# Key halves summed by GpSimd, first loads reordered, stacked rows copied by two engines, second memory projected at a norm

## The reference

```python
def layer0_and_3(x, memory):                     # own weights each
    mp = memory @ W_mem.T                        # memory projection, 256 x 256
    c = softmax(x @ mp.T / sqrt(256)) @ mp
    g = sigmoid(concat(x, c) @ W_gate.T + b_gate)
    return rmsnorm(x + g * c) * norm_w
def layer1(x, ctx):                              # vm: mask that picks expert v or l
    h = rmsnorm(x); q, k, v = split(where(vm, h @ v_qkv, h @ l_qkv))
    x += where(vm, A @ v_dense, A @ l_dense)     # A: causal attention, 16 heads of 16, rotary q, k
    x += cross_attention(rmsnorm(x), ctx)        # 16 heads of 8
    x += where(vm, mlp_v(rmsnorm(x)), mlp_l(rmsnorm(x)))    # 688 hidden
def layer2(x, ctx):
    x += tanh(g1) * latent_attention(layernorm(x), ctx)     # 16 heads of 64, masked keys
    x += tanh(g2) * gelu(layernorm(x) @ W1) @ W2            # 1024 hidden
```

## Time and profile before

| | |
|---|---|
| median of 3 runs | 793.43 us |
| profiled execution | 791.2 us |
| its span | 789.3 us |
| PE, DVE, ACT, POOL busy | 709.3, 387.7, 360.7, 8.6 us |
| mean granted PE clock | 0.95 of full |
| PE's share of the chain that ended last | 79% |

### The profile page before, as it was taken

How to read it: one execution, slowest core, us unless ns; L and a number is a source line. 1 busy time by engine, 2 the same in 40 slices (tenths; PEclk the granted TensorE clock), 3 DMA queues, 4 the chain that set the end, 5 groups by cost and what they waited for, 6 DMA issues and landing times.

```text
span 789.3 us, 13530 instructions
## 1 busy us (share of the span) xinstructions
PE 709.3 (90%) x5816; PEld 557.7 (71%) x5816; DVE 387.7 (49%) x798; ACT 360.7 (46%) x716; POOL 8.6 (1%) x12
## 2 busy tenths in 40 slices
PE   4788898898999999999886979987999999999995
PEld 3667675557987777678774867654689867776893
DVE  0645826637824644152356284366276455433414
ACT  3413453477322566545253245535564345665433
POOL 0010000000000000000001000000000000000000
PEclk9979999599999999999997989979899999999999
DMA  8302000021021000400400020001020400000000
GB/s 323 157 0 81 2 2 28 2 75 74 1 81 81 1 1 2 160 21 7 167 27 1 1 81 2 2 27 56 19 74 1 161 1 2 1 2 1 1 0 27
DMA packets 6555, 34.57 MB, mean 44 GB/s; under 512 B 1504, under 2 KB 2784, under 8 KB 4960
## 3 DMA queue, kind: packets, MB, share of 16 engines
q1 hardware_dynamic: 5056, 26.85, 9.0%
q10 hardware_dynamic: 1440, 6.86, 2.4%
HBM read 32.66 MB, written 1.05 MB: 43 GB/s over the span
## 4 chain that ended last, share of the span: by engine, by line
PE 79%; DVE 10%; ACT 8%; issue 1%; DMA 1%; SPq 0%; ACTq 0%; DVEq 0%
PE ps_B L842 7%; PE ps_A L842 7%; PE ps_B L631 4%; PE ps_A L631 3%; PE ps_B L807 3%; PE ps_A L807 3%; PE ps_B L913 2%; PE ps_A L913 2%; PE ps_B L644 2%; PE ps_A L644 2%; PE ps_A L963 2%; PE ps_B L597 2%; PE ps_B L951 2%; PE ps_A L951 2%; PE ps_B L963 2%; PE ps_B L989 2%
## 5 line engine op out<-in xcount | busy, mean ns | idle before, releaser
L1530 DVE TENSOR_REDUCE max_A<-ps_A 128x2 f32<-128x512 f32 x64 | 39.9, 685 | 23.2 <-PE ps_A L770 13.1
L1530 DVE TENSOR_REDUCE max_B<-ps_B 128x2 f32<-128x512 f32 x64 | 40.4, 685 | 22.0 <-PE ps_B L770 17.0
L631 PE MATMUL ps_B<-q_B,kz_B 128*128 128x256 f32 x264 | 36.8, 299 | 2.2 <-DVE kz_B L1455 1.7
L631 PEld LDWEIGHTS ps_B<-q_B,kz_B 128*128 128x128 f32 x264 | 34.2, 199 | 4.1 <-DVE kz_B L1455 1.9
L807 PE MATMUL ps_B<-q_B,kz_B 64*128 64x256 f32 (+1 forms) x320 | 32.1, 310 | 5.5 <-ACT big_B L1236 2.9
L1232 ACT ACTIVATE big_B<-ps_B,key_bias_B 128x256 f32<-128x256 f32 x64 | 25.0, 474 | 21.5 <-PE ps_B L818 21.5
L1067 ACT ACT_TABLE_LOAD x27 | 34.6, 1283 | 0.5
L1236 ACT ACTIVATE big_B<-ps_B 128x384 f32<-128x384 f32 (+1 forms) x48 | 23.6, 544 | 24.5 <-PE ps_B L818 24.4
L842 PE MATMUL ps_B<-big_B,v_B 128*32 128x256 f32 (+2 forms) x320 | 34.3, 396 | 0.0
L631 PE MATMUL ps_A<-q_A,kz_A 128*128 128x256 f32 x264 | 33.2, 286 | 0.9 <-DVE kz_A L1455 0.8
L807 PEld LDWEIGHTS ps_B<-q_B,kz_B 64*128 64x128 f32 (+1 forms) x320 | 23.5, 194 | 14.9 <-ACT big_B L1236 5.4
(11 more groups left out here) (351 smaller groups left out, 1574.5 us busy)
## 6 DMA issues: line engine op xcount, KB each, us to landing
ffn_w<-in_l1m SPq DMA_DIRECT2D x2, 3072.0 KB, 13.3
ffn_w<-in_l2f SPq DMA_DIRECT2D x2, 3072.0 KB, 9.7
attn_w<-in_l1a SPq DMA_DIRECT2D x2, 2048.0 KB, 9.4
v_B<-in_l1d ACTq DMA_DIRECT2D x2, 1408.0 KB, 5.7
v_A<-in_l1d ACTq DMA_DIRECT2D x2, 1408.0 KB, 5.7
attn_w<-in_l2q SPq DMA_DIRECT2D x2, 1024.0 KB, 4.9
attn_w<-in_l2q SPq DMA_DIRECT2D x4, 512.0 KB, 4.6
v_A<-in_gm SPq DMA_DIRECT2D x2, 640.0 KB, 6.4
```

The costliest lines, as they stand in the source:

```text
L631: last = mm(out, weights(a)[:, at:at + P], L.x_part(i, b), start=(t == 0), stop=(t == len(terms) - 1))
L1530: last = nc.vector.tensor_reduce(mx[:, :, h], L.ps[:, h % 4, :].rearrange("p (q k) -> p q k", q=ST), AX.X, ALU.max)
```

## The change

1. **Key halves.** For cross and latent attention POOL adds the two key halves of each head's exponentials (128 x 256 float32, both inputs in SBUF) into a spare tile (`key_sums`: `xv`, `xl`, and for cross also `xn` and `big2`). `weigh` then has one sum matmul a head in place of two, and waits for POOL's adds between the value matmuls and the sum matmuls. There are 32 adds for a lane and pass. POOL gets an order list, and its memsets stand in it. Self attention stays as it is.
2. **First loads.** Lane A's context, the projection part of the first memory's weights (128 KB, a transfer of its own) and A's sequence go first; const comes fourth; then B's context and sequence, the gate weights, positions and `trig`, which now go into `ffn_w`. One-hot, rotary matmuls and ACT's three copies are moved behind lane A's first norm. The waits for them move to `rotate` and `stack_self`, and the load of the experts' weights into `ffn_w` waits for them.
3. **Stacked rows.** ACT copies banks 0 and 1 of q and k, DVE banks 2 and 3.
4. **Second memory.** `memory_projection(L, 1)` and ACT's `memory_save(L, 1)` come before `sum_squares(L, 5)`, the norm of the GELU layer, and wait for `added(4)`; `ffn_up` waits for the copies, `gm_scores` for `added(5)`.
5. **Orders.** The lists of PE, ACT and DVE are written anew. Lane A's memory stage opens pass 0; from self attention on lane B leads in pass 0 as before, but now it also leads through the experts and latent attention and opens pass 1.

```diff
 (ORDER: PE, ACT and DVE lists replaced)
+    "POOL": [
+        0, 1, 2, 17, 16, 8, 8, 9, 9, 1, 17, 16, 8, 8, 8, 8],
...
+            def key_sums(self, a, i):
+                n = i % (2 * TILES[a])
+                if n < 4:
+                    return self.chunk((self.xv, self.xl)[n // 2], n % 2)
+                return self.chunk(self.xn, n - 4) if n < 6 else self.chunk(self.big2, n - 4)
...  (SP)
+            context(A, 0)
+            memory_weights()
+            sequence(A, 0)
+            sp.dma_start(const[:], const_d).then_inc(const_in.sem, 16)
+            context(B, 0)
+            sequence(B, 0)
+            gate_weights()
+            (positions, then trig into ffn_w, on trig_in)
...
+                else:
+                    sp.wait_ge(trig_ready.sem, 1)
                 sp.dma_start(ffn_w[:], l1m_d).then_inc(weights_in["l1m"].sem, 16)
...  (POOL)
+                def add_halves(L, block):
+                    a, h0, heads = BLOCKS[block]
+                    n0 = a * HEADS + h0
+                    for i in range(heads):
+                        b = i // TILES[a]
+                        if i % TILES[a] == 0 and b >= 2:
+                            wait(*L.pv_done.at(it, BLOCK_BASE[block] + b - 1))
+                        wait(*L.probs_ready.at(it, n0 + i + 1))
+                        p = L.weights(a, i)
+                        nc.gpsimd.tensor_tensor(L.key_sums(a, i), p[:, 0:S], p[:, S:2 * S], ALU.add)\
+                            .then_inc(L.halves_added.sem, 1)
+                        yield
...  (PE, weigh)
-                        for part in range(2):
+                        for part in range(2 if a == SELF else 1):
...
+                        if a != SELF:
+                            pe.wait_ge(*L.halves_added.at(it, n0 - HEADS + (b + 1) * tiles))
+                            for j in range(tiles):
+                                last = mm(strip(j, 1, 0), sums(a, order[b * tiles + j]), L.key_sums(a, b * tiles + j),
+                                          start=False, stop=final, skip_group_check=True)
                         last.then_inc(L.pv_done.sem, 1)
...  (ACT, stacked_self)
-                        for b in range(4):
+                        for b in range(2):
...  (DVE, new, after self_lo)
+                def stacked_self(L):
+                    for tile, stacked, saved in ((L.q[:], L.q_stacked, L.q_ready),
+                                                 (L.kz[:, 0:8 * S], L.k_stacked, L.k_saved)):
+                        dve.wait_ge(*stacked.at(it, 1))
+                        tiles = tile.rearrange("p (c b s) -> p b c s", c=2, b=4)
+                        for b in range(2, 4):
+                            nc.vector.tensor_copy(tiles[:, b], L.ps[:, b, :].rearrange("p (c s) -> p c s", c=2))\
+                                .then_inc(saved.sem, 1)
+                            yield
...  (PE, order of a lane)
+                yield from memory_projection(L, 0)
                 yield from gated_memory(0)
                 yield from sum_squares(L, 0)
+                if it == 0 and L.t == 0:
+                    yield from rotary_tables(L)
...
                 yield from layer_norm_sum(L, 1)
+                yield from memory_projection(L, 1)
                 yield from sum_squares(L, 5)
```

More of the change, by code:

```diff
@@ L182, in build @@
         tanh_gates = sb("tanh_gates", 2)
-        weights_in = {n: signal(f"weights_in_{n}") for n in ("gm0", "gm1", "l1a", "l1c", "l1m", "l2kv", "l2q", "l2f")}
+        weights_in = {n: signal(f"weights_in_{n}") for n in ("gm0", "gm1", "gm0_mem", "l1a", "l1c", "l1m", "l2kv", "l2q", "l2f")}
         const_in = signal("const_in")
         onehot_ready = signal("onehot_ready")
+        trig_in = signal("trig_in")
         trig_done = signal("trig_done")
@@ L232, in __init__ @@
                 self.stat = m("stat", 8)
-                self.inputs_in = s("inputs_in")
+                self.inputs_in = s("inputs_in", 16)
+                self.ctx_in = s("ctx_in", 16)
                 self.down_in = s("down_in", 16)
@@ L296, in __init__ @@
                 self.head_out = s("head_out", 11)
+                self.halves_added = s("halves_added", 32)
                 self.added_done = s("added_done", 5)
@@ L506, in wait, with batch @@
                 pool.sem_inc(pool_waits.sem, 1)
-            for it in range(PAIRS):
-                for L in lanes:
-                    if it:
-                        wait(*L.pv_done.at(it - 1, 16))
-                    nc.gpsimd.memset(L.mask_row[:].bitcast(F32), 0.0).then_inc(L.rows_cleared.sem, 1)
-                for L in lanes:
-                    wait(*L.sq_ready.at(it, 1))
-                    nc.gpsimd.memset(L.v[:, 0:V_AT[LATENT]], 0.0).then_inc(L.v_cleared.sem, 1)
+            def batch(L, it):
+                def add_halves(L, block):
[10 more added lines that the diff above has]
+                        yield
+                if it:
+                    wait(*L.pv_done.at(it - 1, 16))
+                nc.gpsimd.memset(L.mask_row[:].bitcast(F32), 0.0).then_inc(L.rows_cleared.sem, 1)
+                yield
+                wait(*L.sq_ready.at(it, 1))
+                nc.gpsimd.memset(L.v[:, 0:V_AT[LATENT]], 0.0).then_inc(L.v_cleared.sem, 1)
+                yield
+                for block in (1, 2, 3):
+                    yield from add_halves(L, block)
+            weave(ORDER["POOL"], *(chain(*(batch(L, it) for it in range(PAIRS))) for L in lanes))
         @block.tensor
@@ L521, in _, with rotary_tables @@
             mm = nc.tensor.matmul
-            pe.wait_ge(const_in.sem, 80)
-            pe.wait_ge(onehot_ready.sem, 1)
-            for half, table in enumerate((T_COS, T_SIN)):
-                for c in range(ST):
-                    last = mm(lanes[0].half(0, half), lanes[1].big[:, table + c * P:table + (c + 1) * P],
-                              lanes[0].chunk(lanes[0].big, c), start=(c == 0), stop=(c == ST - 1))
-            last.then_inc(trig_done.sem, 1)
+            def rotary_tables(L):
+                pe.wait_ge(trig_in.sem, 32)
+                pe.wait_ge(onehot_ready.sem, 1)
+                for half, table in enumerate((T_COS, T_SIN)):
+                    for c in range(ST):
+                        last = mm(L.half(0, half), ffn_w[:, table + c * P:table + (c + 1) * P],
+                                  onehot[:, c * S:(c + 1) * S], start=(c == 0), stop=(c == ST - 1))
+                last.then_inc(trig_done.sem, 1)
+                yield
             def batch(L, it):
@@ L1053, in _, with rotary_tables @@
             act.dma_start(constb[:], constb_d.bitcast(BF16)).then_inc(const_in.sem, 16)
-            act.wait_ge(const_in.sem, 80)
+            act.wait_ge(const_in.sem, 48)
             fn(tanh_gates[:], vec[:, VEC_GATES:VEC_GATES + 2], ACT.Tanh).then_inc(tanh_ready.sem, 1)
-            act.wait_ge(trig_done.sem, 1)
-            fn(cos[:], lanes[0].half(0, 0), ACT.Copy)
-            fn(fast[:], lanes[1].big[:, T_FAST:T_END], ACT.Copy)
-            fn(sin[:], lanes[0].half(0, 1), ACT.Copy).then_inc(trig_ready.sem, 1)
+            def rotary_tables(L):
+                act.wait_ge(trig_in.sem, 32)
+                fn(fast[:], ffn_w[:, T_FAST:T_END], ACT.Copy)
+                act.wait_ge(trig_done.sem, 1)
+                fn(cos[:], L.half(0, 0), ACT.Copy)
+                fn(sin[:], L.half(0, 1), ACT.Copy).then_inc(trig_ready.sem, 1)
+                yield
             step = Steps(act, act_step)
@@ L1285, in gated_memory @@
                     yield from gm_sigmoid(L, g)
+                yield from memory_save(L, 0)
                 yield from gated_memory(0)
                 yield from rstd(L, 0)
+                if it == 0 and L.t == 0:
+                    yield from rotary_tables(L)
                 yield from rstd(L, 1)
@@ L1316, in batch @@
                 yield from w1_hi(L, 1)
+                yield from memory_save(L, 1)
                 yield from rstd(L, 5)
@@ L1334, in _, with rotary_onehot @@
             stt = nc.vector.scalar_tensor_tensor
-            dve.wait_ge(const_in.sem, 80)
-            for c in range(ST):
-                last = ts(lanes[0].chunk(lanes[0].big, c), pos_i[:], const[:, K_IOTA:K_IOTA + 1], float(c * P),
-                          ALU.subtract, ALU.is_equal)
-            last.then_inc(onehot_ready.sem, 1)
+            def rotary_onehot():
+                dve.wait_ge(trig_in.sem, 32)
+                for c in range(ST):
+                    last = ts(onehot[:, c * S:(c + 1) * S], pos_i, const[:, K_IOTA:K_IOTA + 1], float(c * P),
+                              ALU.subtract, ALU.is_equal)
+                last.then_inc(onehot_ready.sem, 1)
+                yield
+            dve.wait_ge(const_in.sem, 48)
             def lines(tile, n, cols=S):
@@ L1622, in batch @@
                 yield from self_lo(L)
+                yield from stacked_self(L)
                 yield from all_maxima(0)
```

61 lines of the change are left out of this document (38 added, 23 removed), and 43 rows, old and new, of the table ORDER.

## The result

The changed kernel takes **783.48 us** (median, 782.51 to 783.83, 4 runs); the kernel before took 794.58 beside it. The ratio is **0.986, 95% interval 0.982 to 0.990**: 11 us faster, where 28.4 were forecast. The time lies above the forecast's range (756 to 779).

The account below looks back on a forecast made before the run. PE work was taken as the bound in most stretches, DVE's maxima in some. The terms 7 + 15.4 + 5 - 1 + 2 = 28.4 us took 791.2 to 762.8; with the median 2.2 higher, 765 us, range 756 to 779.

Parts of the forecast that it names:

- price of an add: POOL's 128x256 add of two SBUF inputs in cross and latent attention: 0.7 us, between 0.43 and 0.93.
- Latent, 15.4 us forecast: Latent attention: halved sum matmuls save PE 0.48 us in each of 32 steps, all counted, 15.4 us.
- Cross, 5 us forecast: Cross attention: halved sum matmuls save 0.44 us in each of 16 steps, 7.0 us, of which 5 counted.
- The cover: Cross attention: two adds have 1.66 us before their sums are wanted, 0.83 us each, less the signals.
- Rival A: POOL keeps latent but loses cross, by adds of 0.9 to 1.1 us or adds waiting for DVE; 771 us, chance 0.10.
- Rival B: POOL paces cross and latent steps and becomes the bound, slower than before; up to 840 us, chance 0.04.
- Rival C: Less PE work and a new wait lower the clock in more cross stretches; 775 us, chance 0.09.
- Rival D: The early start is absorbed by gate weights, masks or rotary insertion; other edits give 21.4; 772 us, chance 0.07.
- First loads, 7 us forecast: Start: first scores near 9 us instead of 17.11, 8 us sooner, less 1 us for rotary tables; gain 7.
- The rotary insertion: Start: one-hot, four rotary matmuls and three ACT copies between the first lane's two norms cost 1 us.
- Second memory, 2 us forecast: End of each pass: projection moved to the last layer norm gains 1 us per pass, 2 in all.
- Stacked rows, -1 us forecast: Row stacks copied by ACT and DVE: a loss of 1 us, ends +3 and -5, from DVE copies in maxima.

Follow-up runs that it names:

- latent_halves: The changed kernel with key halves for latent attention only, cross having its four sum matmuls a head pair on PE again; 778.20 us, ratio 0.9815.
- dve_adds: The changed kernel with key halves for latent only, its 64 adds on DVE instead of POOL, cross without halves; 774.51 us, ratio 0.976.
- adds_unused_cross: one_half with only the 64 cross adds put back on POOL, their results used by nobody; 775.19 us, ratio 0.979.
- one_half: The changed kernel without POOL's adds or PE's wait for them, one sum matmul a head over the first key half; 768.75 us, ratio 0.969.
- adds_unused: one_half with the 128 POOL adds put back, their results used by nobody and PE not waiting; 782.14 us, ratio 0.988.
- late_clear: The changed kernel with POOL's first clears of the value tiles put behind DVE's one-hot table; 779.32 us, ratio 0.982.
- only_halves: The kernel before with the key halves alone, cross and latent, in its own orders with a fitted POOL list; 781.15 us, ratio 0.985.

## Why the prediction was wrong

**The step that failed** is "price of an add", not by its number but by what it was a price of. An undisturbed add took 0.71 us, where I took 0.7, and PE's waits for POOL came to 1.4 us. I asked only whether the add would be late for PE, and put its effect on DVE and on the clock at nothing in the sum. There the cost fell, 13 us by ratio (0.969 to 0.986): DVE's operations became longer and PE waited for them, and PE's matmuls ran at a lower clock. Two engines that both have idle time do not have the same instants free. Two terms of the sum fail with it.

*Latent, 15.4 us forecast.* Without adds the saved matmuls gave 13 us, 0.41 us a step of the 0.48. With POOL's adds 8.6. The starts of the adds put the period of a step at 2.87 to 3.55 us, where it was 3.48, not always at 3.0. The missing 4 to 5 us come of the adds being on POOL, for on DVE the same adds cost nothing; 2.0 us of them show as PE's longer wait for `max_parts` (6.0 us in latent_halves, 4.0 in dve_adds).

*Cross, 5 us forecast.* The matmuls alone are worth 5; with POOL's adds cross lost 3.6. adds_unused_cross puts the presence of the cross adds alone at 8 us (0.969 to 0.979). The cover that I worked out, 0.83 us an add, was exceeded in the stretch with two-input DVE work (up to 1.3 us), but PE waited little for it: DVE's chain and the clock were the dearer loss.

*Rival A* had the mechanism, the lock on two inputs, at 0.10. Its price was built on adds held up by DVE, 12 x 0.6 us, in cross alone. Missing were the other direction, DVE held up by adds, and the small operations in latent of which I had said nothing since they take 0.17 us. A short operation on the path can pay nearly the whole length of the instruction it waits for (0.70 us for 0.18). *Rival B*, POOL as the bound, did not occur: POOL was busy 107 us. *Rival C*, the clock, was right as a fact, 0.938 for 0.950, with 0.82 and 0.84 in two cross windows that had 1.00 and 0.91; but its reason does not hold: one_half (0.953) shows that it does not come of fewer matmuls, and adds_unused (0.944), without PE's new wait, that it does not need that wait. *Rival D* is partly true: the first loads gave 4.0 us at self attention's first projection, but its last sum matmul in pass 0 started at 126.3 us, before at 125.4. No run undid the first loads alone, so what they are worth in the end is open.

*First loads, 7 us forecast, 4.0 at the first projection.* The transfers came as said: first projection 4.21 us (4 foreseen), first scores 10.11 (9). The rotary insertion had been put at 1 us; it took 3, of which late_clear gives 1.9 back. (The estimate "twice 0.6 us" for the one-hot misread its row, which has 0.62 us for both operations.) I had priced DVE's one-hot by its length in the kernel before, where POOL did nothing beside it.

*Second memory, 2 us forecast:* 2 to 3 measured. *Stacked rows, -1 us forecast:* not told apart from nothing. All other edits together gave 6 us of the 8. Adding the terms up failed too: the halves gave 12 us on the kernel before and the other edits 6 without the halves, but together they gave 11, by ratio (0.986).

## What to carry to other kernels

When work is moved to an idle GpSimd, look at what VectorE does in the same microseconds, not at GpSimd's idle time: an instruction of either that shares the ports holds the other's up until it ends, as the rows here show, and short operations on the critical chain lose most. The test is cheap: run the new instructions with the critical engine not waiting for them, and a memset in their place with every wait kept; the two tell presence from lateness. And try the busier engine first, since 0.42 us an add on a VectorE that is half busy was free in latent attention where 0.71 us on an idle GpSimd cost 4; in cross attention it was not.

## What the runs showed that I had not expected

- A POOL memset, which reads nothing, let `tensor_tensor` pass (0.69 us beside it) and held a `tensor_scalar` until about its own end (2.24 us for two that take 0.61, done at 32.94 us; the memset ended at 32.79).
- An earlier start of 1.9 us gave 3 to 4 us at the end in two kernels, with a higher granted clock in both. The clock of one and the same kernel (late_clear) varied between executions by 0.013, and the time by 4 us with it; in others (one_half, latent_halves: 0.950 to 0.953) it hardly moved.
- The 64 latent adds on POOL cost 4 us (0.9815 against 0.976), by the unused adds 7; the 64 cross adds cost 8. POOL was busy 46 us with the first and 54 with the second, and their prices are not clear of each other's intervals; that what runs beside them matters, more than their number, shows in only_halves, where the same 128 adds leave 12 us of gain and not 5.
